# A transformer block on one Trainium2 core: the fifth weight piece's low halves on GpSimd, and the first block in another order

## What is computed

```python
x = L0_attn_x                                  # (4, 1024, 512)
xn = _layernorm(x, axis=-1)
x = x + _L0_attn_ref(xn, ...) + _L0_ffn_ref(xn, L0_ffn_w_gate, L0_ffn_w_up, L0_ffn_w_down)

# attention branch: ternary weights, 16 heads of 32, chunks of 128, decaying state S
scale = 1.0 / jnp.clip(jnp.mean(jnp.abs(w)), 1e-05, None)
q = jnp.clip(jnp.round(w * scale), -1.0, 1.0) / scale
...
scores = jnp.einsum('bhtd,bhsd,hts->bhts', qi, ki, mask)
intra = jnp.einsum('bhts,bhsd->bhtd', scores, vi)
cross = jnp.einsum('bhtd,ht,bhde->bhte', qi, lam_t, S)
...
# feed-forward branch, hidden width 2048
gated = jax.nn.silu(gate) * up
return jnp.einsum('bsh,dh->bsd', gated, w_down)
```

## Time and profile before

| | us |
|---|---|
| median of 3 runs | 1362.36 |
| lowest and highest | 1362.04, 1362.48 |
| the profiled execution | 1361.45 |
| its span in the profile | 1359.7 |
| TensorE busy | 1334.2 (98%) |
| VectorE busy | 924.6 (68%) |
| ScalarE busy | 486.5 (36%) |
| GpSimd busy | 67.5 (5%) |

### The profile page before, as it was taken

How to read it: one execution, slowest core, us unless ns; L and a number is a source line. 1 busy time by engine, 2 the same in 40 slices (tenths; PEclk the granted TensorE clock), 3 DMA queues, 4 the chain that set the end, 5 groups by cost and what they waited for, 6 DMA issues and landing times.

```text
span 1359.7 us, 21928 instructions
## 1 busy us (share of the span) xinstructions
PE 1334.2 (98%) x8332; PEld 721.3 (53%) x8332; DVE 924.6 (68%) x1886; ACT 486.5 (36%) x915; POOL 67.5 (5%) x88
## 2 busy tenths in 40 slices
PE   5899999999999999999999999999999999999999
PEld 3455555555455554555545555555545555455554
DVE  6988995576655766657766677657775576755655
ACT  7964633233233332333323233223332233232331
POOL 5600000000000000000000000000000000000000
DMA  8242234113431145211351113510145112431121
GB/s 314 83 142 67 87 73 120 26 32 67 111 88 28 30 79 124 53 32 40 71 140 35 29 40 70 148 40 26 38 85 132 32 30 49 94 94 32 32 48 47
DMA packets 193767, 98.72 MB, mean 73 GB/s; under 512 B 127104, under 2 KB 179328, under 8 KB 192000
## 3 DMA queue, kind: packets, MB, share of 16 engines
q1 hardware_dynamic: 193376, 97.30, 28.3%
q10 hardware_dynamic: 288, 0.01, 0.0%
HBM read 34.35 MB, written 8.39 MB: 31 GB/s over the span
## 4 chain that ended last, share of the span: by engine, by line
PE 94%; DVE 3%; ACT 1%; DMA 1%; SPq 1%; issue 1%; POOL 0%; DVEq 0%; POOLq 0%
PE bank L517 89%; PE bank L559 2%; PE bank L586 1%; PE bank L588 1%; DVE wg_lo L1292 0%; SPq L935 0%; DMA xin<-x 0%; ACT wg_lo L1142 0%; DMA k_stack<-k_parts 0%; DVE arena L861 0%; DMA q_stack<-q_parts 0%; DVE arena L747 0%; DVE xt L748 0%; DVE wd_lo L1292 0%; DVE wu_lo L1292 0%
## 5 line engine op out<-in xcount | busy, mean ns | idle before, releaser
L517 PE MATMUL bank<-wd_hi,arena 128*128 128x512 f16 x1024 | 317.0, 379 | 0.0
L517 PE MATMUL bank<-xt,wg_hi 128*128 128x512 f16 x1024 | 306.5, 381 | 3.6 <-ACT ql L728 1.6
L517 PE MATMUL bank<-xt,wu_hi 128*128 128x512 f16 x1024 | 304.6, 379 | 0.0
L517 PE MATMUL bank<-xt,wg_lo 128*128 128x512 f16 x512 | 195.0, 381 | 0.0
L517 PE MATMUL bank<-wd_lo,arena 128*128 128x512 f16 x512 | 194.0, 379 | 0.0
L517 PE MATMUL bank<-xt,wu_lo 128*128 128x512 f16 x512 | 194.0, 379 | 0.0
L517 PEld LDWEIGHTS bank<-wd_hi,arena 128*128 128x128 f16 x1024 | 100.2, 98 | 115.3
L789 DVE TENSOR_TENSOR sm<-bank,mask 128x512 f32<-128x512 f32 x128 | 88.1, 688 | 105.4 <-PE bank L559 105.3
L517 PEld LDWEIGHTS bank<-xt,wu_hi 128*128 128x128 f16 x1024 | 99.0, 98 | 104.4 <-issue 0.5
L517 PEld LDWEIGHTS bank<-xt,wg_hi 128*128 128x128 f16 x1024 | 98.2, 98 | 103.5 <-issue 4.6
L673 ACT ACTIVATE sm_hi<-sm 128x512 f16<-128x512 f32 x128 | 80.1, 626 | 193.5 <-DVE sm L789 193.5
(11 more groups left out here) (200 smaller groups left out, 1492.2 us busy)
## 6 DMA issues: line engine op xcount, KB each, us to landing
k_stack<-k_parts SPq DMA_DIRECT2D x192, 64.0 KB, 2.2
q_stack<-q_parts SPq DMA_DIRECT2D x192, 64.0 KB, 2.2
arena<-x SPq DMA_DIRECT2D x8, 1024.0 KB, 5.9
out<-arena SPq DMA_DIRECT2D x32, 256.0 KB, 2.4
xin<-x SPq DMA_DIRECT2D x30, 256.0 KB, 4.5
stage<-up_t SPq DMA_DIRECT2D x4, 1024.0 KB, 5.3
stage<-down_t SPq DMA_DIRECT2D x4, 1024.0 KB, 4.9
stage<-gate_t SPq DMA_DIRECT2D x3, 1024.0 KB, 4.8
```

The lines of the kernel that those rows point to most:

```text
L517: last = e.matmul(dst, a, b, start=start and n == 0, stop=stop and n == len(lhs) - 1)
```

## The change

GpSimd makes the two low halves of piece 4, in two instructions each: it multiplies the piece with its scale where it lies in `stage`, and then subtracts the high half. Two new semaphores count this, `cut` hands out GpSimd's count for piece 4, and the counts of the other even pieces are lowered by its two parts. `FIRST_ORDER` is replaced for all five engines; `STEADY_ORDER` stays as it is.

```diff
 "DVE": [
-        ('UL', 3), ('RD', 0), ('SO', 1), ('FT', 2), ('U', 4), ('RD', 1), ('WT', 4), ('U', 5), ('HD', 0), ('WT', 5),
-        ('UL', 4), ('WN', 0), ('UL', 5), ('FT', 3), ('K', 0), ('U', 6), ('Q', 0), ('WC', 4, 0), ('WC', 4, 1), ('WC', 5, 0),
+        ('RD', 0), ('RD', 1), ('FT', 0), ('FT', 1), ('U', 5), ('WT', 4), ('HD', 0), ('WT', 5), ('WN', 0), ('UL', 4),
+        ('K', 0), ('UL', 5), ('U', 6), ('FT', 2), ('FT', 3), ('Q', 0), ('WC', 5, 0), ('UL', 6), ('V', 0), ('SC', 0, 0),
...
     "POOL": [
-        ('S4', 0), ('RD', 2), ('RD', 3), ('RD', 4), ('RD', 5), ('RD', 6), ('MS', 0), ('NR', 0), ('ST', 0), ('NR', 1),
-        ('ST', 1),
+        ('S4', 0), ('RD', 2), ('RD', 3), ('RD', 4), ('MS', 0), ('RD', 5), ('RD', 6), ('WC', 4, 0), ('WC', 4, 1), ('NR', 0),
+        ('ST', 0), ('NR', 1), ('ST', 1),
     ],
...
 POOL_TERNARY = 2
+POOL_LOW = (4,)
...
+    s_pool_lo, s_pool_scaled = sem("piece_lo_pool"), sem("piece_scaled_pool")
...
-        return s_wlo[n % 2], before(n) + -(-tiles * parts_of(n) // HPQ)
+        if n in POOL_LOW:
+            return s_pool_lo, sum(parts_of(m) for m in POOL_LOW if m < n) + -(-tiles * parts_of(n) // HPQ)
+        return s_wlo[n % 2], before(n) - sum(parts_of(m) for m in POOL_LOW if m < n and m % 2 == n % 2) + -(-tiles * parts_of(n) // HPQ)
...
+                elif kind == "WC":
+                    i = it[2]
+                    e.wait_ge(s_whi[n % 2], before(n) + i + 1)
+                    hi_part, lo_part = piece_parts(n, i)
+                    w = piece_raw(n, i)
+                    e.tensor_scalar(w, w, ws[:, n:n + 1], 1.0, ALU.mult, ALU.mult).then_inc(s_pool_scaled, 1)
+                    e.wait_ge(s_pool_scaled, sum(parts_of(m) for m in POOL_LOW if m < n) + i + 1)
+                    e.tensor_tensor(lo_part, w, hi_part, ALU.subtract).then_inc(s_pool_lo, 1)
```

## The result

The changed kernel takes 1365.52 us (median of 15 runs, 1364.67 to 1366.38), the kernel before 1362.96 in the same session (15 runs, 1361.14 to 1364.48). The ratio is 1.002 with a 95% interval of 1.0012 to 1.0027: 2.6 us slower, which is just inside the 0.2% (2.7 us) that I called no change. The forecast of 1366.2 was 0.7 too high. It stood for 3.8 us over the kernel before, whose median has since come out 0.6 higher (1362.36, then 1362.96), so as a change the forecast was 1.2 too high. The profiled execution took 1365.13 with a span of 1363.4, 3.7 us more than before; the profiled execution of the kernel before (1361.45) was 1.5 faster than that kernel's median here, so the two profiles show more difference than the medians.

A forecast was written before the change was run, and what follows sets the result against it. TensorE was taken to bound the kernel, only its idle time counting. O(0,0) 5.6 us late, -0.8 for stack waits and -1.0 for the tail gave +3.8, so 1366.2 us as median, range 1359.2 to 1369.2.

The forecast's parts named there:

- What bounds: TensorE sets the time; only its idle time, some 8 us in the first block and 1.5 in the second, can be won.
- Turns: GpSimd passes and VectorE's SBUF-only operations alternate exclusively; a pass costs VectorE up to that whole pass.
- The subtraction: GpSimd's two-input subtraction over 1024 columns for piece 4: taken as 1.98 us, bounds 1.04 to 3.
- Part 2: First block: SO0 moves back behind U3 on VectorE, so GpSimd's ternary work starts at 44.0, 9 us later.
- the walk: First block stepped through with alternating turns: U5 at 51.85, K0 at about 63.3, O(0,0) 5.6 us late.
- Part 3: VectorE's WN, some 3.2 us, ahead of UL4: UL4 ends at 70.75, G6's SiLU 4.8 us late, gap 6.5 before G7.
- From the SiLU to O(0,0): First block, G6's SiLU to O(0,0): some 10.7 us with the new VectorE list, against 9.9 before.
- The stack waits: TensorE's stack waits at 84.64 and the next like it close, as TensorE comes later: -0.8 us.
- The tail: End of first block: XT and TH2 earlier, so the q_stack wait at 212.67 shrinks: -1.0 us, bounds -1.6 and +0.5.
- Cover holds: Rival: turns cost half, hidden under UL4's wait for tile 4's high half; 1359.0 to 1360.6 us; chance 0.26.
- part of it: Rival: SiLU of G6 at 68 to 69, sum within 1.5 us of zero, 1361 to 1364 us; chance 0.17.
- SyncE's case: Rival: GpSimd ends piece 4 after about 83, stacks late, SC(1,0) waits 1 to 3 us more; 1367 to 1369; chance 0.05.

The follow-up runs named there:

- e1: Changed kernel with the two low halves of piece 4 made by VectorE again, new orders kept; 1364.74 us, ratio 1.0015 to the kernel before.
- e2: Kernel before, in its old orders, with only the two low halves of piece 4 moved to GpSimd; 1366.54 us, ratio 1.0028.
- e4: Changed kernel with GpSimd's RD6 and piece 4's low halves each cut into eight passes of 512 columns; 1369.45 us, ratio 1.0047 to the kernel before.
- e11: Changed kernel, GpSimd making piece 4's low halves for 32 of every 512 columns, zeros written behind its first item; 1364.57 us, ratio 1.0011.
- e12: Kernel before with only the last items of the first block in the changed kernel's order; 1362.26 us, ratio 0.9999.
- e7: Changed kernel with SO0 ahead of U2, mask work behind RD5, WN behind D(0,0), and piece 4 on VectorE; 1365.01 us, ratio 1.0015.
- e6: Changed kernel with SO0 ahead of U2, mask work behind RD5, and WN behind D(0,0), piece 4 on GpSimd; 1366.29 us, ratio 1.0030.
- e9: Changed kernel with WN behind D(0,0), piece 4 on VectorE, and the scores' low half ahead of WC(4,1) and WC5; 1367.66 us, ratio 1.0031.
- e10: Changed kernel with WN behind D(0,0) and the scores' low half ahead of WC5, piece 4 on GpSimd; 1366.43 us, ratio 1.0023.
- e3: Changed kernel with WN moved on VectorE from ahead of UL4 to behind D(0,0); 1364.12 us, ratio 1.0009 to the kernel before.
- e8: Changed kernel, GpSimd making piece 4's low halves for 32 of every 512 columns, zeros written ahead of its first item; 1366.68 us, ratio 1.0031.

## Why the prediction was right, and where it wasn't

An account of the profiles shows where the changed kernel's 3.7 us lie: TensorE's gaps of 0.15 us and more from 22 to 240 us, and what the lower clock cost (5 us stretches, each with 1 minus its granted clock, the last stretch of the kernel left out).

| profile | gaps to 100 | gaps 100 to 240 | lower clock | sum | against before | span against before |
|---|---|---|---|---|---|---|
| before | 6.76 | 1.33 | 0 | 8.09 | | |
| changed | 8.36 | 0 | 3.40 | 11.76 | +3.7 | +3.7 |
| e1 | 8.84 | 0.39 | 1.70 | 10.93 | +2.8 | +3.3 |
| e2 | 7.39 | 0.79 | 3.40 | 11.58 | +3.5 | +4.0 |

For the other kernels the sum misses the span by up to 2.4 us (e4), so I use it for these alone. It is an account of profiles, not a cause: a wait that is shortened by a slow stretch ahead of it counts as won, and the slow stretch as lost. In e11 the lower clock costs where VectorE waits for V0 (2.38), in e1 VectorE doesn't wait for V0 at all, and the clock's 1.70 us stand in the sum just the same. And the medians are 2.6 apart, not 3.7.

By the steps of the prediction:
- **What bounds** held: the second block's two waits closed, and from the third block's first K (+3.4) to the end (+3.7) nearly nothing changed.
- **Turns** held: UL4 ends 0.53 after a pass of GpSimd (69.04 after 68.51), UL5 0.56 after its subtraction, WC(5,0) 1.08 after the next one (76.63 after 75.55). By the Trainium skill ("SBUF — State Buffer", section "SBUF: two separate sides") GpSimd and VectorE share a pair of ports under an exclusive lock. These rows agree, and so does e4, where the pieces interleave.
- **The subtraction**, taken as 1.98, takes 2.13 when it isn't held up, and 2.43 when it is. My 1.98 was 0.15 below. The estimate of 2.25 by "GPSIMD Engine Reference" of the Trainium skill, section 3.1, was as near, 0.12 above.
- **Part 2 and the walk** to K0 held: 44.15 for 44.0, U5 at 51.93 for 51.85, K0 at 63.56 for 63.3.
- **Part 3**, WN ahead of UL4, was the right place and too large: UL4 ended at 69.04, not 70.75. I had the last of WN's three operations wait for piece 4's first pass and UL4 for the subtraction behind it. The first two did wait (1.36 and 2.00), but the last, at 66.93, got its turn at once (0.68), the pass waited for it, and UL4 waited for the end of that pass (68.51) only. So the SiLU lost 3.1 us, not 4.8, and the gap ahead of G7 was 4.5, not 6.5.
- **From the SiLU to O(0,0)** I had 10.7 us, and it took 11.85. Two things stand there that this term doesn't have. UL5 waits for the first subtraction (1.94 instead of 0.68, so 1.26), the turn that I had put on UL4, ahead of the SiLU. And VectorE stands 0.62 us for V0, since TensorE came back at the lower clock, which the prediction doesn't have at all. The two misses, -1.7 and +1.15, cancel for the most part because the same turn moved from one term to the other; that no more than 0.5 is left of them is luck. So O(0,0) at +5.06 looks like the forecast's +5.6.
- **The stack waits**, -0.8: O(0,0) at +5.06 became +5.02 at the second block's first K (206.34 for 201.32), so nothing was given back there. The wait at 84.64 did close; what took its 0.8 us I haven't traced.
- **The tail**, -1.0: the delay shrank from +5.02 to +3.4 at the third block's first K, 1.6. The size was at my lower bound. Of the reason e12 says that it is half right at most: with the new tail the waits close, but new ones ahead of D(3,3) and PJ cost 1.2 of the 1.5 us. That the changed kernel doesn't have these, because its TensorE comes 5 us late, is likely and not shown.
- **Rivals.** "Cover holds" and "part of it" are out for the changed kernel as built (G7's gap of 4.5), the late stacks of SyncE's case came true in e4 only, and there through the landing of the writes.
- **The number.** The sum of +3.8 is the profiles' +3.7, but the profile before was of an execution 1.5 us below the median. The runs say +2.6, and 1366.2 came as near as 0.7 partly because the kernel before ran 0.6 slower in the later session. That is luck too.

**What the prediction overrated** is the move. It made GpSimd's turns with piece 4 part of the wait ahead of the SiLU and of the way to O(0,0). With the move undone (e1) the SiLU of tile 6 still starts at 68.29, so 2.3 of its 3.1 us of delay come from the new orders, where WN meets RD6. Undone in the new orders it gives back 0.8 us (e1), with its turns taken out 0.9 (e11), with GpSimd early 1.3 (e7 against e6), and in the old orders it costs 3.8 (e2); between e9 and e10 it is 1.2 the other way, inside the error. The new orders without the move cost 2.0 (e1). WN's place is worth some 1.4, measured with the move in (e3); what the rest of the 2.0 is, no run separates. Each of these differences but e2's and e1's to the kernel before is about as large as its error. That the parts add up to more than the whole (3.8 and 2.0 against 2.6) means that the move costs less in the new orders than in the old ones.

**What stays open.** Why TensorE's clock fell in one profile and not in another with the same gaps. The kernel before has gaps of 0.51 and 1.65 at 56.5 and 58.5 with a clock of 1.00 throughout, while e2 and e12, with the same gaps to 0.01 us (a third of a microsecond later), have 0.88 and 0.78 between 55 and 65 us. How the 2.6 us divide among the move, WN's place and the rest of the orders is not settled, since the parts are as large as the errors. And no version beat the kernel before.

## What to carry to other kernels

In a stretch where several engines are each nearly full, an item's delay at one point says little about the end: of the 4 to 6 us that WN's place and the order around the scores gave at O(0,0), the time showed between nothing and a third, as the next queue (a stack, the scores' low half) took over. Before moving work to an engine that looks idle, list which operations of the neighbour meet it there and what stands behind each, and price the waits by these. And put into such a sum what TensorE does after a gap of some microseconds, for it can come back at half speed, as here from 70 to 75 us.

## What the runs showed of the hardware that I hadn't expected

- **The clock after a gap.** After 4.51 us without work (the changed kernel) TensorE was granted the lower level for the next 5 us and more: G7's twelve matmuls took 5.1 us instead of 2.6. After 3.92 us it happened in e1, e8 and e11 with different lengths (1.7, 1.7 and 3.4 us lost by the account), and after e10's 4.38 the clock was 0.50 from 88 to 90 us. Over the timed runs, the mean granted clock was 0.999 or 1.0 in 75 of the 85 runs of the kernel before beside e1 to e12, and 0.998 or less in 12 of 15 of the changed kernel. Runs of the changed kernel with 0.999 took 1365.06 on average (3 runs), those with 0.996 or 0.997 1365.63 (11 runs); for e1 it was 1364.43 (7) and 1365.30 (4), for e3 1363.27 (0.999 and 1.0, 4 runs) and 1364.61 (7). The 0.6 us between the changed kernel's two groups is about VectorE's 0.62 for V0, but three runs are few.
- **Cutting GpSimd's instructions helps its neighbour and not itself.** 2048 columns in four pieces beside a busy VectorE took 3.81 us instead of 1.97 (e4), while VectorE's SBUF operations from WN to UL5 got shorter (UL4 0.85 instead of 1.28, UL5 1.11 instead of 1.94).
- **Small writes behind large loads land later.** The stack of K1, three writes of 64 KB, landed 2.4 to 3.1 us after the issue in the changed kernel, where a load of 1 MB had gone out 4.6 us ahead of the first; 4.1 to 5.5 in e10, where it was 3.4 us ahead; and 6.0 to 6.3 in e4, where two loads had gone out 4.3 and 4.0 us ahead.
- **GpSimd's subtraction** with an f16 result and 1024 columns takes 2.13 us where no VectorE operation holds it, 1.9 times the 1.12 of the multiply over the same columns ahead of it.
